# Attention and slot FFN in one kernel: the start of the first head reordered, its weights' and values' low parts moved among its scores

## The chip, the cores and the metric

The kernel runs on one core of a Trainium2 chip. The metric is the device time of one launch in microseconds, median of three runs.

## The reference

Attention over 8 batches of 1024 tokens with 8 heads of width 128, a residual and layer norm, a soft mixture of slots with its residual and layer norm behind it. Everything is fp32.

```python
q, k, v = (einsum('bim,mhd->bhid', x, w) for w in (wq, wk, wv))
q, k = rope(q), rope(k)                       # even*cos - odd*sin, even*sin + odd*cos
s = einsum('bhid,bhjd->bhij', q, k) / 128     # masked above the diagonal
o = einsum('bhij,bhjd->bhid', softmax(s), v)
x = layernorm(x + einsum('bhid,hdm->bim', o, wo))
x = layernorm(x + slot_ffn(x, gamma_x, gamma_slot, slot_embeds, w1, w2))
```

## The kernel before, in words

One block computes attention for 64 heads (8 batches x 8), a second block the FFN. The change lies in the first block and there in what precedes head 0 and in the step of head 0.

**Number format.** Matmuls run on fp32r operands in two parts: a high part (a copy rounded to fp32r, made by ScalarE with `ACT.Copy`, "hi") and a low part (the original less the high part, a subtraction on VectorE or GpSimd, "lo"). `matmul_split` (lines 53 to 57) is three matmuls: hi x hi, hi x lo, lo x hi. x, the projection weights, k, q, the values and the turned probabilities are all split so.

**A head.** k and q are projected from x (L55 to L57 into `ps_slot`), copied to SBUF (`raw_k` L516, `raw_q` L527 into `unrot`), and rotated: a product with the cosine table (`mul_cos_k` on GpSimd L417, `mul_cos_q` on VectorE L668, half by half), a swap of the upper and lower 64 partitions by two transfers on SyncE's queue (`swap`, L340), a product of the swapped copy with the sine table (`mul_sin`, GpSimd L423), a sum (`rotate_add`, GpSimd L431), then high part (`split_hi`, ScalarE L534) and low part (`split_lo`, GpSimd L439). For head 0 VectorE does part of it: sine product of k at L808, both sums at L813, both low parts at L819. The values are x times wv times wo, the product of the two weight matrices is made once (L1048, `wvo_all`, high part L593, low part L834), and the values of two heads come from one projection; head numbers -2 and -1 stand for those of the first heads (`split_v_hi` L541, `split_v_lo` L694). They are summed in `ps_turn` and `ps_y`, as the slots of `ps_slot` are taken.

**A step.** Scores of one head come in slots "s4", "s7", "s6", "s5", "s10", "s32", named by the row tiles in them. VectorE adds the mask and takes the negative row maximum (`rowmax`, L649), ScalarE takes exp (L506) into `probs`, TensorE turns the probabilities ("turn", L904, L916, L921, into two banks of `ps_turn`), ScalarE and VectorE split them (L551 to L562, L676 to L686), TensorE multiplies them with the values into `ps_y`. Each engine runs a fixed program, `step(head)`, which mixes the end of the head before, this head and the projection of the next. Order on each engine is order of the code; engines meet by semaphores alone.

**The start.** x of batch 0 arrives in halves on SyncE's queue (L390), then the two rotation tables (L394), which wait for x. ScalarE's queue brings the first two heads' k and q weights (L576), and, behind a wait for x, the values' and output weights (L579, L580) and the other six heads' weights (L583) into `probs`, which holds all raw weights before the first exp writes it. The six heads' weights are split into `kept.w` by ScalarE (`split_rest_hi`, L571) and VectorE (`split_rest_lo`, L801), before the first step. TensorE's first step waits for both low parts of q and k (`lo_made`) and for both of the values (`v_lo`, by `free_slot(v_lo, before, -2, -2, 2)`). Its turn "6a" waits for VectorE's low part of "7b", whose bank it takes (`turn("6a", head, ("7b", head))`).

`y_head` and `y_sum` hold a head's output and the sum over heads; both are first written when head 0's output is scaled, in step 1.

## Time and profile before

| | |
|---|---|
| median of 3 runs | 1671.52 us (1671.47 to 1673.33) |
| the profiled execution's own time | 1672.75 us |
| its span, first to last instruction | 1670.7 us |
| TensorE busy | 1625.1 us, 97% of the span, 10452 matmuls |
| GpSimd busy | 1413.7 us, 85% |
| VectorE busy | 1244.0 us, 74% |
| ScalarE busy | 1214.0 us, 73% |
| mean granted TensorE clock | 0.995 |

Busy shares are averages over the whole span. In the page's 40 slices (41.8 us each) TensorE reads 4 tenths in the first slice and 9 in nearly all the others; the granted clock reads 8 in the first and 9 (90% or more) in all others. In a timeline row, the first number is the start in us from the first instruction, the second the duration, and the bracket tells how long the engine had been idle before it and what ended that. Rows with ACTq or SPq are issues of transfers, not the transfers.

### The profile page before, as it was taken

The page shows a single profiled execution, that of the slowest core. Times are in us where ns is not written, and L with a number is a line of the kernel's source. Part 1 is how long each engine was busy: PE and PEld are TensorE (multiplying, and loading weights), DVE is VectorE, ACT ScalarE, POOL GpSimd, SP SyncE. Part 2 cuts the span into 40 slices and gives each one's busy share as a digit, 9 for nine tenths or more (in the row PEclk, how much of TensorE's full clock was granted, in tenths as well). Part 3 has the DMA queues.
Part 4 walks back from the last instruction along what each step waited for, and adds up shares of the span by engine and source line. Part 5 has one row for each costly group of instructions (what it writes and reads, how often), then busy time and mean ns, then how long its engine had stood idle before and what let it go on. Part 6 is the DMA issues. An engine that isn't in the chain of part 4 may idle for free. (4 is left out here: it accounts for less than half of the span.)

```text
span 1670.7 us, 29885 instructions
## 1 busy us (share of the span) xinstructions
PE 1625.1 (97%) x10452; PEld 1471.7 (88%) x10452; DVE 1244.0 (74%) x2899; ACT 1214.0 (73%) x2427; POOL 1413.7 (85%) x797
## 2 busy tenths in 40 slices
PE   4999999999999999999999999999999997999997
PEld 4899999999999999999999999999999986999997
DVE  5787778777877777778777877787777777677775
ACT  3877777777777777777777777777777764665664
POOL 4799989998999899998999899989998975777884
PEclk8999999999999999999999999999999999999999
DMA  5222232223222322232223222322232323123212
GB/s 151 77 76 75 77 99 71 74 75 98 74 75 74 100 73 75 74 99 76 77 77 102 77 77 77 102 77 76 77 89 76 89 77 102 45 67 96 68 33 58
DMA packets 69763, 134.10 MB, mean 80 GB/s; under 512 B 19312, under 2 KB 38000, under 8 KB 69616
## 3 DMA queue, kind: packets, MB, share of 16 engines
q1 hardware_dynamic: 67856, 130.10, 28.9%
q10 hardware_dynamic: 1760, 2.10, 0.4%
q8 instruction: 85, 1.39, 0.4%
q14 instruction: 62, 0.51, 0.1%
HBM read 56.36 MB, written 8.70 MB: 39 GB/s over the span
## 5 line engine op out<-in xcount | busy, mean ns | idle before, releaser
L506 ACT ACTIVATE probs<-ps_slot,neg_max 128x640 f32<-128x640 f32 (+7 forms) x512 | 381.1, 746 | 154.2 <-DVE neg_max L649 154.2
L649 DVE CUSTOM_DVE_ANT_0 ps_slot<-ps_slot,causal 128x640 f32<-128x640 f32 (+7 forms) x512 | 383.0, 769 | 132.7 <-PE ps_slot L57 132.4
L904 PE MATMUL ps_turn<-ident,probs 128*128 128x128 f32 x2048 | 279.2, 274 | 2.3 <-DVE pt_high L676 1.2
L55 PE MATMUL ps_slot<-k,q 128*128 128x512 f32 (+4 forms) x768 | 274.9, 358 | 6.5 <-DVE v L694 5.1
L57 PE MATMUL ps_slot<-k,q 128*128 128x512 f32 (+4 forms) x768 | 264.9, 345 | 0.0
L56 PE MATMUL ps_slot<-k,q 128*128 128x512 f32 (+4 forms) x768 | 263.1, 343 | 0.0
L904 PEld LDWEIGHTS ps_turn<-ident,probs 128*128 128x128 f32 x2048 | 232.8, 140 | 21.8 <-issue 2.1
L676 DVE TENSOR_TENSOR pt_split<-ps_turn,pt_split 128x512 fp32r<-128x512 f32 x256 | 175.3, 685 | 93.4 <-ACT pt_split L551 93.4
L439 POOL TENSOR_TENSOR q<-rot_q,q 128x1024 fp32r<-128x1024 f32 x63 | 152.2, 2416 | 52.6 <-ACT q L534 52.6
L423 POOL TENSOR_TENSOR swapped_k<-swapped_k,rope 128x1024 f32<-128x1024 f32 x63 | 152.4, 2420 | 42.6 <-DMA swapped_k<-unrot_k 42.5
L417 POOL TENSOR_TENSOR rot_k<-unrot_k,rope 128x1024 f32<-128x1024 f32 x64 | 154.7, 2417 | 16.4 <-ACT unrot_k L516 13.8
L55 PEld LDWEIGHTS ps_slot<-k,q 128*128 128x128 f32 x768 | 146.6, 191 | 20.8 <-issue 6.9
L423 POOL TENSOR_TENSOR swapped_q<-swapped_q,rope 128x1024 f32<-128x1024 f32 x64 | 159.2, 2487 | 6.1 <-DMA swapped_q<-unrot_q 6.1
L431 POOL TENSOR_TENSOR rot_k<-rot_k,swapped_k 128x1024 f32<-128x1024 f32 x63 | 151.8, 2409 | 9.0
L56 PEld LDWEIGHTS ps_slot<-k,q 128*128 128x128 f32 x768 | 146.4, 191 | 14.1
L431 POOL TENSOR_TENSOR rot_q<-rot_q,swapped_q 128x1024 f32<-128x1024 f32 x63 | 150.5, 2389 | 9.0
L57 PEld LDWEIGHTS ps_slot<-k,q 128*128 128x128 f32 x768 | 145.7, 190 | 13.9
L439 POOL TENSOR_TENSOR k<-rot_k,k 128x1024 fp32r<-128x1024 f32 x63 | 152.0, 2413 | 1.8 <-ACT k L534 1.8
L551 ACT ACTIVATE pt_split<-ps_turn 128x512 fp32r<-128x512 f32 x256 | 147.0, 603 | 1.9 <-PE ps_turn L904 1.9
L455 POOL TENSOR_TENSOR y_sum<-y_sum,y_head 128x1024 f32<-128x1024 f32 x55 | 132.0, 2400 | 18.7 <-issue 18.4
L1268 POOL TENSOR_TENSOR comb<-logits,row_b 128x512 f32<-128x512 f32 x64 | 96.8, 1551 | 48.4 <-DMA row_b<-r_rows 48.3
L676 DVE TENSOR_TENSOR pt_high<-ps_turn,pt_high 128x512 fp32r<-128x512 f32 (+2 forms) x192 | 100.5, 551 | 46.5 <-ACT pt_high L551 46.5
(198 smaller groups left out, 4426.1 us busy)
## 6 DMA issues: line engine op xcount, KB each, us to landing
swapped_k<-unrot_k SPq DMA_DIRECT2D x128, 256.0 KB, 3.6
swapped_q<-unrot_q SPq DMA_DIRECT2D x128, 256.0 KB, 3.6
inv_b<-inv_rows SPq DMA_DIRECT2D x64, 512.0 KB, 4.7
y_t<-y_sum SPq DMA_DIRECT2D x8, 512.0 KB, 5.4
x_raw<-y_t SPq DMA_DIRECT2D x8, 512.0 KB, 4.1
unrot_q<-in_L_attn_x SPq DMA_DIRECT2D x8, 512.0 KB, 5.4
row_b<-r_rows SPq DMA_DIRECT2D x16, 256.0 KB, 3.6
x_raw<-x_cols SPq DMA_DIRECT2D x7, 512.0 KB, 5.3
```

What stands on the lines that cost most here:

```text
L55: pe.matmul(out, stat_hi, mov_hi, start=start, stop=False, skip_group_check=True)
L56: pe.matmul(out, stat_hi, mov_lo, start=False, stop=False, skip_group_check=True)
L57: return pe.matmul(out, stat_lo, mov_hi, start=False, stop=stop, skip_group_check=True)
L417: pool.tensor_tensor(rot[1][:, :], unrot[1][:, :], kept.rope[:, 0, :], ALU.mult).then_inc(cos_made[1], 1)
L423: pool.tensor_tensor(swapped[which][:, :], swapped[which][:, :], kept.rope[:, 1, :], ALU.mult).then_inc(sin_made[which], 1)
L431: pool.tensor_tensor(rot[which][:, :], rot[which][:, :], swapped[which][:, :], ALU.add).then_inc(rotated[which], 1)
L439: pool.tensor_tensor(out[:, 1, :], rot[which][:, :], f32(out[:, 0, :]), ALU.subtract)\
L506: act.activation(probs_tile(t), score_tile(name, head, i), ACT.Exp, scale=-1.0, bias=neg_max[:, head.par, t:t + 1], accum_out=sums[:, head ...
L551: last = act.activation(hi, src, ACT.Copy)
L649: dve.tensor_tensor_reduce(tile, tile, causal[:, T - WIDTH[t]:T], -1.0, UNSEEN, ALU.add, ALU.min, neg_max[:, head.par, t:t + 1]).then_inc( ...
L676: last = dve.tensor_tensor(lo, src, f32(hi), ALU.subtract)
L904: last = pe.transpose(bank[:, at:at + P], probs_tile(t)[:, j * P:(j + 1) * P], ident[:, :])
```

## The change

It does six things, all before or in the first step:

- SyncE issues the rotation tables right behind x, without a wait.
- ScalarE loads its table by a small Exp (of a constant into `inv`, which is overwritten later), waits for x half by half and splits it, and issues the values' and output weights after that.
- The six other heads' k and q weights are loaded into `y_head` and `y_sum`, issued after the copy of q of head 0; their high parts are made in step 0 between exp of "s6" and the high part of head 1's k, their low parts in step 0 on VectorE after the row maxima of "s6" and of "s5".
- VectorE makes the low part of k before the sum of q, then the low part of q and the cosine product of head 1's q; the values' low parts come behind these and in step 0, behind the row maximum of "s7".
- ScalarE copies q of head 1 before the high part of the second values.
- TensorE's order is the same; its waits for the values' low parts move from the first scores to the first turn (one) and to step 1 (both).

```diff
@@ sync
-            sp.wait_ge(first_x_landed[1], 16)
             for i, table in enumerate((rope_c, rope_s)):
                 sp.dma_start(kept.rope[:, i, :], table).then_inc(rope_landed[i], 16)
@@ scalar
+        rest_raw = {"k": y_head, "q": y_sum}
...
-            act.wait_ge(first_x_landed[1], 16)
-            act.dma_start(w_raw["v"], wv.rearrange("d h m -> d (h m)")).then_inc(w_landed["v"], 16)
-            act.dma_start(w_raw["o"].rearrange("p (h m) -> p h m", h=H), wo.rearrange("h d m -> d h m"))\
-               .then_inc(w_landed["o"], 16)
-            for n, w in (("k", wk), ("q", wq)):
-                act.dma_start(w_raw[n][:, FIRST_HEADS * D:], w[:, FIRST_HEADS:H, :].rearrange("m h d -> m (h d)"))\
-                   .then_inc(rest_landed, 16)
+            act.wait_ge(consts, 1)
+            act.activation(inv[:, 0, :], kept.minus_half[:, :], ACT.Exp)
             for half in range(2):
                 act.wait_ge(first_x_landed[half], 16)
                 act.activation(kept.x_t[0][:, 0, half_cols(half)], kept.x_raw[:, half_cols(half)], ACT.Copy)\
                    .then_inc(first_x_hi, 1)
+            act.dma_start(w_raw["v"], wv.rearrange("d h m -> d (h m)")).then_inc(w_landed["v"], 16)
+            act.dma_start(w_raw["o"].rearrange("p (h m) -> p h m", h=H), wo.rearrange("h d m -> d h m"))\
+               .then_inc(w_landed["o"], 16)
             first, second = Head(0, 0, heads), Head(0, 1, heads)
             raw_k(first)
             raw_q(first)
+            for n, w in (("k", wk), ("q", wq)):
+                act.dma_start(rest_raw[n][:, 0:(H - FIRST_HEADS) * D], w[:, FIRST_HEADS:H, :].rearrange("m h d -> m (h d)"))\
+                   .then_inc(rest_landed, 16)
             act.wait_ge(wvo_made, 1)
             act.activation(wvo_part(0), both_y, ACT.Copy).then_inc(wvo_hi, 1)
             split_hi(1, first)
             raw_k(second)
             split_v_hi(first.step(-2))
             split_hi(0, first)
+            raw_q(second)
             split_v_hi(first.step(-1))
-            raw_q(second)
-            split_rest_hi("k", WK_HI, 1.0)
-            split_rest_hi("q", WQ_HI, 1.0 / P)
...
                 exp("s6", head)
+                if is_step(head, 0):
+                    split_rest_hi("k", WK_HI, 1.0)
+                    split_rest_hi("q", WQ_HI, 1.0 / P)
                 split_hi(1, after)
@@ vector, step
                 rowmax("s7", head)
+                if is_step(head, 0):
+                    split_v_lo(before)
...
                 rowmax("s6", head)
+                if is_step(head, 0):
+                    split_rest_lo("k", WK_HI, WK_LO, 1.0)
...
                 rowmax("s5", head)
+                if is_step(head, 0):
+                    split_rest_lo("q", WQ_HI, WQ_LO, 1.0 / P)
@@ vector, start
+            first_split_lo(1)
             first_add(0)
-            first_split_lo(1)
+            first_split_lo(0)
+            mul_cos_q(second)
             split_v_lo(first.step(-2))
-            first_split_lo(0)
-            split_v_lo(first.step(-1))
-            mul_cos_q(second)
-            split_rest_lo("k", WK_HI, WK_LO, 1.0)
-            split_rest_lo("q", WQ_HI, WQ_LO, 1.0 / P)
@@ tensor, step
+                if is_step(head, 1):
+                    pe.wait_ge(v_lo, 2)
                 weigh_high(before, (0, 1))
-                free_slot(v_lo, before, -2, -2, 2)
+                if not is_step(head, 0):
+                    free_slot(v_lo, before, -2, -2, 2)
...
+                if is_step(head, 0):
+                    pe.wait_ge(v_lo, 1)
                 turn_shared(before, head)
```

VectorE from the product of the two weight matrices to the first row maxima, before (`rot` are the rotated k and q, `w_all` the six heads' weights):

```order
L813 TENSOR_TENSOR rot_k<-rot_k,swapped_k 128x1024 [waits cos_made_k,sin_made_k]
L834 TENSOR_TENSOR wvo_all<-ps_y,wvo_all 128x1024 [waits wvo_hi]
L813 TENSOR_TENSOR rot_q<-rot_q,swapped_q 128x1024 [waits cos_made_q,sin_made_q]
L819 TENSOR_TENSOR k<-rot_k,k 128x1024 [waits hi_made_k]
L694 TENSOR_TENSOR v<-ps_turn,v 128x1024 [waits v_hi]
L819 TENSOR_TENSOR q<-rot_q,q 128x1024 [waits hi_made_q]
L694 TENSOR_TENSOR v<-ps_y,v 128x1024 [waits v_hi]
L668 TENSOR_TENSOR rot_q<-ps_slot,rope 128x512 [waits filled_q,lo_made_q]
L668 TENSOR_TENSOR rot_q<-ps_slot,rope 128x512 [waits raw_made_q]
L801 SCALAR_TENSOR_TENSOR w_all<-probs,w_all 128x6x128 [waits rest_hi] x2
L649 ISA ps_slot,neg_max<-ps_slot,causal 128x640 [waits filled_s4,consts]
```

And now:

```order
L827 TENSOR_TENSOR k<-rot_k,k 128x1024 [waits hi_made_k]
L821 TENSOR_TENSOR rot_q<-rot_q,swapped_q 128x1024 [waits cos_made_q,sin_made_q]
L827 TENSOR_TENSOR q<-rot_q,q 128x1024 [waits hi_made_q]
L670 TENSOR_TENSOR rot_q<-ps_slot,rope 128x512 [waits filled_q,lo_made_q]
L670 TENSOR_TENSOR rot_q<-ps_slot,rope 128x512 [waits raw_made_q]
L696 TENSOR_TENSOR v<-ps_turn,v 128x1024 [waits v_hi]
L651 ISA ps_slot,neg_max<-ps_slot,causal 128x640 [waits filled_s4,consts]
```

The low part of k stands before the sum of q, the low part of q before both low parts of the values, and the two weight parts have left the place before the first row maximum.

VectorE in step 0, now, from the row maximum of "s7" on (lines 651 are row maxima, 730 the weights' low parts, 678 the probabilities' low parts):

```order
L651 ISA ps_slot,neg_max<-ps_slot,causal 128x1024 [waits filled_s7]
L651 ISA neg_max 128x1
L696 TENSOR_TENSOR v<-ps_y,v 128x1024 [waits v_hi]
L688 TENSOR_TENSOR pt_high<-ps_turn,pt_high 128x128 [waits turn_hi]
L651 ISA ps_slot,neg_max<-ps_slot,causal 128x896 [waits filled_s6]
L730 SCALAR_TENSOR_TENSOR w_all<-y_head,w_all 128x6x128 [waits rest_hi]
L651 ISA ps_slot,neg_max<-ps_slot,causal 128x768 [waits filled_s5]
L730 SCALAR_TENSOR_TENSOR w_all<-y_sum,w_all 128x6x128 [waits rest_hi]
L678 TENSOR_TENSOR pt_high<-ps_turn,pt_high 128x4x128 [waits turn_hi]
```

The second values' low part and the two weight parts now stand between the row maxima and the low part of "7b".

ScalarE's start, now (line 582 splits x, 591 loads the six heads' weights):

```order
L576 DMA probs<-in_L_attn_wk 128x256
L576 DMA probs<-in_L_attn_wq 128x256
L579 ACT_TABLE_LOAD
L579 ACTIVATE inv<-minus_half 128x8 [waits consts]
L582 ACTIVATE x_t<-x_raw 128x512 [waits first_x_landed0]
L582 ACTIVATE x_t<-x_raw 128x512 [waits first_x_landed1]
L584 DMA probs<-in_L_attn_wv 128x1024
L585 DMA probs<-in_L_attn_wo 128x8x128
L516 ACTIVATE unrot_k<-ps_slot 128x1024 [waits filled_k]
L527 ACTIVATE unrot_q<-ps_slot 128x512 [waits filled_q]
L527 ACTIVATE unrot_q<-ps_slot 128x512 [waits cos_made_q]
L591 DMA y_head<-in_L_attn_wk 128x768
```

Before, the four transfers of weights stood ahead of the table load and of x's split.

## Rows read from the trace of the kernel before

**Rows 1.** Busy times in one long stretch: us, then busy (x instructions) per engine, clock.

```profile
60.00:1340.00 1280.00, 1280.00 (x8003) 1156.13 (x8003) 967.27 (x2075) 990.06 (x2076) 1153.34 (x486) 1.00 0.30 81
```

**Rows 2.** Timeline of the start, all engines, 5 to 12 us.

```profile
5.35 0.36 ACTq L579 DMA_DIRECT2D probs<-in_L_attn_wv  x1
...
5.84 0.43 DVE L794 SCALAR_TENSOR_TENSOR w_all<-probs,w_all 128x256 fp32r<-128x256 f32 x1
...
8.34 1.28 ACT L587 ACT_TABLE_LOAD   x1 [8.34 <-issue]
9.63 1.15 ACT L587 ACTIVATE x_t<-x_raw 128x512 fp32r<-128x512 f32 x2
10.29 1.29 DVE L826 TENSOR_TENSOR x_t<-x_raw,x_t 128x512 fp32r<-128x512 f32 x2 [4.03 <-ACT x_t L587]
...
11.13 0.77 PE L55 MATMUL ps_slot<-x_t,w_all 128*128 128x512 f32 x1 [11.13 <-DVE x_t L826]
```

**Rows 3.** The same timeline, k and q of head 0 and GpSimd beside them.

```profile
21.73 2.52 POOL L423 TENSOR_TENSOR swapped_q<-swapped_q,rope 128x1024 f32<-128x1024 f32 x1 [4.12 <-DMA swapped_q<-unrot_q]
...
22.05 1.06 ACT L534 ACTIVATE k<-rot_k 128x1024 fp32r<-128x1024 f32 x1 [3.08 <-DVE rot_k L813]
...
25.43 1.22 DVE L819 TENSOR_TENSOR k<-rot_k,k 128x1024 fp32r<-128x1024 f32 x1
...
26.73 2.35 POOL L417 TENSOR_TENSOR rot_k<-unrot_k,rope 128x1024 f32<-128x1024 f32 x1 [2.47 <-DVE k L819]
...
27.70 2.46 DVE L819 TENSOR_TENSOR q<-rot_q,q 128x1024 fp32r<-128x1024 f32 x1
...
29.03 3.35 POOL L423 TENSOR_TENSOR swapped_k<-swapped_k,rope 128x1024 f32<-128x1024 f32 x1
```

**Rows 4.** Durations of two VectorE lines over the whole run, ns min/median/max.

```profile
L801 DVE SCALAR_TENSOR_TENSOR w_all<-probs,w_all x2: 946/1690/2435, 33.3 to 35.6; 128x768 fp32r<-128x768 f32 x2
...
L712 DVE TENSOR_TENSOR x_t<-x_raw,x_t x14: 689/2218/2394, 82.3 to 1117.2; 128x512 fp32r<-128x512 f32 x14
```

**Rows 5.** The same timeline, first scores to the turn "6a".

```profile
31.21 1.27 DVE L668 TENSOR_TENSOR rot_q<-ps_slot,rope 128x512 f32<-128x512 f32 x2
...
31.39 0.61 PE L55 MATMUL ps_slot<-k,q 128*128 128x320 f32 x1 [5.05 <-DVE v L694]
...
32.42 1.57 ACT L571 ACTIVATE w_all<-probs 128x768 fp32r<-128x768 f32 x2
32.52 2.38 POOL L431 TENSOR_TENSOR rot_k<-rot_k,swapped_k 128x1024 f32<-128x1024 f32 x1
...
33.28 3.31 DVE L801 SCALAR_TENSOR_TENSOR w_all<-probs,w_all 128x768 fp32r<-128x768 f32 x2 [0.80 <-ACT w_all L571]
...
36.51 0.82 DVE L649 CUSTOM_DVE_ANT_0 ps_slot<-ps_slot,causal 128x640 f32<-128x640 f32 x1
36.91 2.36 POOL L423 TENSOR_TENSOR swapped_q<-swapped_q,rope 128x1024 f32<-128x1024 f32 x1 [2.01 <-DMA swapped_q<-unrot_q]
...
37.42 0.79 ACT L506 ACTIVATE probs<-ps_slot,neg_max 128x640 f32<-128x640 f32 x1 [3.44 <-DVE neg_max L649]
...
38.36 0.33 PE L921 MATMUL ps_turn<-ident,probs 128*128 128x128 f32 x1 [2.47 <-ACT probs L506]
...
45.55 0.89 PE L904 MATMUL ps_turn<-ident,probs 128*128 128x128 f32 x6 [1.18 <-DVE pt_high L676]
```

**Rows 6.** Busy times by stretch as in rows 1; the granted clock is the third last.

```profile
31.00:36.00 5.00, 4.50 (x12) 3.44 (x12) 4.20 (x5) 2.06 (x3) 3.76 (x2) 0.51 0.48 112
...
40.00:42.00 2.00, 2.00 (x6) 1.57 (x6) 1.16 (x2) 0.60 (x3) 1.78 (x1) 0.50 0.04 8
```

**Rows 7.** Stretches again (last two: DMA share, GB/s), and an issue with us to landing.

```profile
8.00:9.00 1.00, 0.00 (x0) 0.00 (x0) 0.00 (x0) 0.66 (x1) 0.00 (x0) 1.00 1.02 422
...
19.00:20.00 1.00, 1.00 (x6) 0.84 (x5) 0.46 (x1) 0.00 (x0) 0.00 (x0) 1.00 1.02 266
...
probs<-in_L_attn_wq ACTq DMA_DIRECT2D x1, 384.0 KB, 8.4
```

More of the change, by code:

```diff
@@ L571, in split_rest_hi @@
                 act.activation(kept.w[:, FIRST_HEADS:H, part, :],
-                               w_raw[n].rearrange("p (h d) -> p h d", h=H)[:, FIRST_HEADS:H, :],
+                               rest_raw[n][:, 0:(H - FIRST_HEADS) * D].rearrange("p (h d) -> p h d", d=D),
                                ACT.Copy, scale=scale).then_inc(rest_hi, 1)
@@ L723, in split_slots, with split_rest_lo @@
                                          ALU.mult, ALU.subtract).then_inc(se_lo, 1)
+            def split_rest_lo(n, hi, lo, scale):
+                raw_w = rest_raw[n][:, 0:(H - FIRST_HEADS) * D].rearrange("p (h d) -> p h d", d=D)
+                dve.wait_ge(rest_hi, ("k", "q").index(n) + 1)
+                dve.scalar_tensor_tensor(kept.w[:, FIRST_HEADS:H, lo, :], raw_w, scale,
+                                         f32(kept.w[:, FIRST_HEADS:H, hi, :]), ALU.mult, ALU.subtract)\
+                   .then_inc(w_lo[n], 1)
             def step(head):
@@ L796, in split_first_w @@
                    .then_inc(w_lo[n], 1)
-            def split_rest_lo(n, hi, lo, scale):
-                raw_w = w_raw[n].rearrange("p (h d) -> p h d", h=H)[:, FIRST_HEADS:H, :]
-                dve.wait_ge(rest_hi, ("k", "q").index(n) + 1)
-                dve.scalar_tensor_tensor(kept.w[:, FIRST_HEADS:H, lo, :], raw_w, scale,
-                                         f32(kept.w[:, FIRST_HEADS:H, hi, :]), ALU.mult, ALU.subtract)\
-                   .then_inc(w_lo[n], 1)
             def first_sin_k():
```

## The prediction

> **What bounds the kernel now.** I read the busy table of long stretches first. From 60 to 1340 us TensorE is busy 1280 of 1280 us at its full clock, while VectorE, ScalarE and GpSimd have room [rows 1]. Nothing there waits for a date of the start, so a microsecond saved before that stretch is a microsecond at the end, and the change touches only what lies before it. Then the timeline of the start. TensorE's first matmul is at 11.13 [rows 2], it stands still from about 26.3 to 31.39, and its last wait on the way to the steady part ends at 45.55, where it goes on with head 0's "6a" turn [rows 5]. I forecast two dates: first scores (31.39 now) and that turn (45.55 now).
>
> **The change, part by part.** Sums are made against the profiled execution (span 1670.7, execution 1672.75, which is 1.23 above the median of 1671.52); the saving is taken off the median. Dates "after" are mine.
>
> *x split as it lands, table at once.* Both halves of x have landed at 5.35, when ScalarE issues the transfer that waits for them. It then issues four, loads its table (1.28) and splits x only at 9.63; VectorE's part starts at 10.29 and TensorE 0.84 later [rows 2]. After, table and split are done by about 5.9. VectorE still has q's first weights to split, until 5.84 + 0.43 = 6.27 [rows 2], so it starts on x at 6.27 instead of 10.29: **4.02 us earlier**, first matmul near 7.1. Bounds: the rotation tables now follow x at once and share the engines with q's first weights. Those landed at about 5.5; they may come 0.0 to 0.6 later, and that goes one for one into this date. I take 0, since the tables stand behind x in their own queue. The values' and output weights are issued about 6 instead of 5.35; TensorE wants them near 12.0, and a wait there of a microsecond meets an idle stretch, so nothing.
>
> *The six other heads' weights come later.* Their transfers (768 KB) are now issued right behind the copy of q, when the half swap of q has just been issued. One queue alone moved 266 GB/s (19 to 20 us), two together 422 (8 to 9 us) [rows 7]. If two queues share 422 evenly, the swap (2 x 256 KB) needs 2.5 us for what takes 2.0 alone. Bounds: 0 and 3.9 us (the same weights took 8.4 us to land in company [rows 7], a swap 4.4). I take 0.3, as the pairing at 8 to 9 us is nearest. GpSimd then starts on q's sine product at 21.73 - 4.02 + 0.3 = 18.0.
>
> *The low parts of k and q, reordered.* These VectorE operations read two inputs from SBUF, and here the trace has a warning. The k low part took 1.22 with GpSimd idle; q's took 2.46: it began at 27.70, GpSimd's product ran until 29.08, and the rest is 1.1; GpSimd's next operation then took 3.35 instead of 2.4 [rows 3]. The first weight low part took 2.44 and the second 0.95, the first beside a GpSimd addition until 34.90; the x low parts took up to 2.39 [rows 4, 5]. So whoever comes second waits for the whole operation of the other. The Trainium skill states that rule ("SBUF — State Buffer", section "Who interferes with whom"): a VectorE instruction with two SBUF inputs and a GpSimd one that reads SBUF exclude each other, by order of issue. The trace agrees; without the rule the sum would be the second rival's. With these waits:
> - k: its sine product and sum keep their 4.02, high part 18.03 to 19.1. The low part finds GpSimd busy from 18.0 to 20.4 and ends at 20.4 + 1.1 = 21.5.
> - q: sum 21.4 to 22.6 (GpSimd's cosine product of head 1 waits for it and runs 22.6 to 25.0), high part 22.7 to 23.75, low part behind GpSimd, 25.0 + 1.1 = 26.1.
> - The scores no longer wait for the values' second low part, so **first scores at 26.15 instead of 31.39: 5.2 earlier**.
>
> *Step 0.* VectorE takes the cosine of head 1 (1.27, to 27.3), the values' low part (1.2, to 28.45), then the row maximum of tile 4 (0.8) at 28.4; exp (0.8 + 0.2), and the turn of tile 4 at 30.2 instead of 38.36: 8.1 earlier [rows 5]. This is the largest lead: two weight low parts (3.31) [rows 5] have left the way and the gap before the scores is shorter. Then it is given back. Tile 7's maximum and exp run 29.4 to 31.8, the values' second low part stands before tile 6's maximum, and exp of tile 6 ends at 34.2 (each of these 1.0 to 1.2). ScalarE now splits the weights (1.57 [rows 5], 34.15 to 35.7), and head 1's k comes after. VectorE's k weight low part starts at 35.0. GpSimd: the swap of head 1's q, copied at 27.3, lands 4.4 later, product to 34.1, sum to 36.4; the low part ends at 36.4 + 0.9 = 37.3. Tile 5's maximum to 38.2. GpSimd's next (k low part) has 37.3 to 39.6, so the q weight low part ends at 40.5; then the first piece of turn "7b" (0.6), and TensorE gets its bank at **41.15 instead of 45.55: 4.4 earlier**. Against an undisturbed 0.95 each, the two weight low parts take 2.8 more here. Bounds of this step: 1.1 less if the weights' parts fall into gaps of GpSimd, 1.2 more if one meets a whole operation.
>
> *TensorE's clock.* It had idled 5.05 us before 31.39, and the granted clock of 31 to 36 was 0.51, about 1.2 GHz; at 40 to 42 it was 0.50, although the engine was busy, behind 2.5 idle us before 38.36 [rows 5, 6]. Now TensorE runs out of work near 35.9 and waits to 41.15, 5.2 us, so I expect 1.2 GHz once more, but in a stretch where TensorE itself is the bound: half of 3 us (the shorter low stretch) to half of 4.5 (the longer) are lost, 1.5 to 2.2; the other bound is 0, if the clock holds. I take 1.5, the shorter, for part of it falls in the wait. The low clock of the scores in exchange may vanish; that is in no term, since VectorE's chain sets the dates there.
>
> Sum: 4.4 - 1.5 = **2.9 us faster**, 1671.5 - 2.9 = **1668.6**. About 0.2%, 3.3 us, is what a measurement of this kernel can tell from no change, so this is a gain just under it.
>
> **Rivals.**
> 1. *The order on GpSimd flips.* If q's swap lands after k's low part has begun at 19.1, that is 1.4 us later than undisturbed, k goes first, GpSimd runs q's sine product to 22.7 and head 1's cosine product straight on to 25.0, and q's sum waits for it: 26.1. High part 27.15; GpSimd meanwhile does the sine product of head 1's k until 28.5, and q's low part ends at 29.6. Scores at 29.65, 3.5 later than forecast: 0.6 slower than before, **1672.1** (1671.5 to 1672.7). For it: the trailing weights share the engines with just this swap. "DMA: Bandwidth & Descriptors" of the Trainium skill, section "Issuing engines are not separate DMA queues", says that queues of several engines end on the same DMA engines; rows 7 show that two together still move more than one. Against it: 1.4 is nearly three times the 0.5 worked out for even shares. Chance 0.13.
> 2. *No exclusion worth the name.* If the four low parts run in their 0.95 to 1.2, k ends 20.3, q 23.9, scores 24.0, and the turn comes 7 us earlier: less 1.5 of clock, **1666.0**. Against it: rows 3 and 4. Chance 0.10, with the case that the parts fall into gaps and the clock holds.
> 3. *Slower.* The swap of q waits behind the weights altogether and lands 3.9 us late, as the 8.4 of rows 7 would have it. q's sine product to 24.1, cosine to 26.4, sum 27.5, sine of k to 29.9, q's low part 31.0: scores at 31.05 as before, but step 0 still holds the weights' low parts and the cold turn, 15.0 us against 14.2 and 1.5 of clock: 2.0 slower, **1673.5**. It decides from about 2.5 us of delay on; beyond 5 it would cost over 0.2%. Chance 0.07.
> 4. *The start is not earlier.* q's first weights land so late behind the tables that x's split gains 2 instead of 4: **1670.5**. Chance 0.05. It lies in the range.
>
> **How the numbers follow.** The forecast has 0.65. Its own range: clock loss 0 to 2.2 and first weights 0 to 0.6 late, steps of GpSimd +-1.1: gains of 1.0 to 4.6. The range adds rival 1's nearer half: 1666.8 to 1671.6, leaving out rival 2, half of 1 and 3. Faster by over 0.2%: four tenths of the forecast (0.26, where the clock holds or the low parts find gaps) and rival 2: 0.36. Slower by over 0.2%: the tail of rival 3: 0.03. Within: 0.61.
>
> **What would show it.** x's high part at 5 to 6 and the first matmul near 7.1. q's sine product on GpSimd before k's low part, and k's low part near 2.4 long. q's low part near 2.3. Scores at 26.2. Weight low parts over 1.5 each inside step 0. Turn "6a" near 41.2 behind some 5 idle us, then matmuls of 0.43 per 512 columns for about 3 us. First scores later than 28 would make the forecast wrong by rival 1; low parts of 1.2, or a full clock after the wait, by rival 2.

## The result, and the profile after it

The change was forecast to save 2.9 us; it cost about 2 (1.97 by the medians, 2.3 by the ratio).

| | before | after |
|---|---|---|
| median of 19 runs each, on the same chips | 1672.37 us | 1674.34 us |
| ratio after / before | | 1.0014, 95% interval 1.0007 to 1.002 |
| the profiled execution's own time | 1672.75 us | 1674.33 us |
| its span | 1670.7 us | 1672.2 us |
| mean granted TensorE clock | 0.995 | 0.991 |

The loss of 0.14% is real, as the interval lies above 1, but less than the 0.2% that the prediction took as the limit of what can be told. The three runs of before that the forecast was set against (1671.52) were a little below the median of 19.

Three dates tell where it came from: TensorE's first scores, its turn "6a", and a **mark** behind it, the first group of seven turns in step 1, from where TensorE is full. I use the mark in every run below, since behind it the programs are alike: from the mark to the last projection of the attention, near 1340 us, it is 1288.1 us in all thirteen kernels of this document.

| us | first matmul | first scores | turn "6a" | mark | span |
|---|---|---|---|---|---|
| before | 11.13 | 31.39 | 45.55 | 53.77 | 1670.7 |
| forecast | 7.1 | 26.15 | 41.15 | 50.87 | |
| after | 7.07 | 30.24 | 45.92 | 55.44 | 1672.2 |

(The forecast's mark is 53.77 less the forecast saving of 2.9.) The first matmul came where it was expected. Of its 4.06 us of lead 1.15 were left at the scores, none at turn "6a", and at the mark the program was 1.67 late. The busy row of the long stretch answers to [rows 1]: nothing there took the delay up.

```profile
60.00:1340.00 1280.00, 1280.00 (x8004) 1156.12 (x8003) 967.22 (x2074) 990.05 (x2076) 1152.89 (x486) 1.00 0.30 81
```

The timeline of the changed kernel, all engines, from the start to the mark; the columns are those of [rows 2]. It answers to [rows 2, 3, 5].

```profile
4.40 0.63 ACT L582 ACTIVATE x_t<-x_raw 128x512 fp32r<-128x512 f32 x1 [1.24 <-DMA x_raw<-x_cols]
...
5.39 0.63 ACT L582 ACTIVATE x_t<-x_raw 128x512 fp32r<-128x512 f32 x1 [0.36 <-DMA x_raw<-x_cols]
...
5.90 0.43 DVE L809 SCALAR_TENSOR_TENSOR w_all<-probs,w_all 128x256 fp32r<-128x256 f32 x1
6.24 1.29 DVE L834 TENSOR_TENSOR x_t<-x_raw,x_t 128x512 fp32r<-128x512 f32 x2
...
7.07 0.77 PE L55 MATMUL ps_slot<-x_t,w_all 128*128 128x512 f32 x1 [7.07 <-DVE x_t L834]
...
12.10 0.35 ACTq L591 DMA_DIRECT2D y_head<-in_L_attn_wk  x1
12.49 0.50 ACTq L591 DMA_DIRECT2D y_sum<-in_L_attn_wq  x1
...
13.20 1.12 SPq L341 DMA_DIRECT2D swapped_q<-unrot_q  x2
...
18.75 1.06 ACT L534 ACTIVATE k<-rot_k 128x1024 fp32r<-128x1024 f32 x1 [3.18 <-DVE rot_k L821]
...
19.84 1.23 DVE L827 TENSOR_TENSOR k<-rot_k,k 128x1024 fp32r<-128x1024 f32 x1
...
20.52 2.80 POOL L423 TENSOR_TENSOR swapped_q<-swapped_q,rope 128x1024 f32<-128x1024 f32 x1 [6.95 <-DMA swapped_q<-unrot_q]
...
23.28 2.33 POOL L417 TENSOR_TENSOR rot_k<-unrot_k,rope 128x1024 f32<-128x1024 f32 x1
23.35 3.35 DVE L821 TENSOR_TENSOR rot_q<-rot_q,swapped_q 128x1024 f32<-128x1024 f32 x1 [2.28 <-POOL swapped_q L423]
25.57 3.32 POOL L423 TENSOR_TENSOR swapped_k<-swapped_k,rope 128x1024 f32<-128x1024 f32 x1
26.73 1.06 ACT L534 ACTIVATE q<-rot_q 128x1024 fp32r<-128x1024 f32 x1 [4.05 <-DVE rot_q L821]
...
27.82 2.16 DVE L827 TENSOR_TENSOR q<-rot_q,q 128x1024 fp32r<-128x1024 f32 x1 [1.12 <-ACT q L534]
...
30.24 0.60 PE L55 MATMUL ps_slot<-k,q 128*128 128x320 f32 x1 [7.19 <-DVE q L827]
...
40.30 1.04 DVE L730 SCALAR_TENSOR_TENSOR w_all<-y_head,w_all 128x768 fp32r<-128x768 f32 x1 [1.90 <-ACT w_all L571]
...
42.02 2.34 POOL L439 TENSOR_TENSOR k<-rot_k,k 128x1024 fp32r<-128x1024 f32 x1 [1.49 <-ACT k L534]
...
42.15 3.03 DVE L730 SCALAR_TENSOR_TENSOR w_all<-y_sum,w_all 128x768 fp32r<-128x768 f32 x1
...
45.10 1.14 DVE L678 TENSOR_TENSOR pt_high<-ps_turn,pt_high 128x512 fp32r<-128x512 f32 x2
...
45.92 1.51 PE L909 MATMUL ps_turn<-ident,probs 128*128 128x128 f32 x6 [4.63 <-DVE pt_high L678]
...
55.44 0.93 PE L909 MATMUL ps_turn<-ident,probs 128*128 128x128 f32 x7
```

Read it from the top. x is split at 4.40 and 5.39, VectorE follows at 6.24, TensorE at 7.07. Then look at the bracket of the row at 20.52: GpSimd waited 6.95 us for the half swap of q. The copy of q had ended at 13.17, so the swap landed 7.35 us behind it; before, it was 4.48 (17.25 to 21.73 [rows 3]). The three rows of issues show that the swap was not even first: ScalarE issued both transfers of weights at 12.10 and 12.49, while its copy of q was still running, and SyncE, which waits for the end of the copy, issued the swap at 13.20. Meanwhile k's low part had run (19.84, undisturbed in 1.23), so GpSimd's product began after it. At 23.28 GpSimd goes straight on to head 1's cosine product, and the sum of q, which is on the path, begins 0.07 later and takes 3.35 instead of 1.23: it waits for the whole of the other. q's low part at 27.82 meets a third product. Last, the q weights' low part (3.03) lies over a GpSimd operation of 2.34, and TensorE waits 4.63 us behind it at 45.92.

The stretches of the changed kernel; the last three columns are the granted clock, the DMA share and GB/s. They answer to [rows 6, 7].

```profile
16.00:17.00 1.00, 1.00 (x6) 0.70 (x4) 0.77 (x1) 0.00 (x0) 0.00 (x0) 1.00 1.06 410
17.00:18.00 1.00, 0.24 (x2) 0.00 (x0) 0.97 (x2) 0.00 (x0) 0.00 (x0) 1.00 1.10 280
18.00:19.00 1.00, 0.00 (x0) 0.00 (x0) 1.00 (x2) 0.25 (x1) 0.00 (x0) 1.00 0.92 217
19.00:20.00 1.00, 0.09 (x1) 0.10 (x1) 1.00 (x2) 1.00 (x2) 0.00 (x0) 1.00 0.12 33
25.00:35.00 10.00, 4.76 (x14) 4.07 (x15) 7.30 (x8) 3.96 (x7) 7.07 (x3) 0.50 0.23 57
42.00:49.00 7.00, 3.08 (x15) 3.11 (x16) 5.53 (x11) 3.38 (x10) 2.34 (x1) 0.51 0.00 0
```

The DMA engines are full until 19, at 410 GB/s from 16 to 17 and at 217 from 18 to 19, when the end of the weights (the second transfer lands 6.6 us after its issue, about 19.1) and the swap are left. A tail follows: a share of 0.12 from 19 to 20 is on average two of sixteen engines still at work. The swap's landing, at 20.52, lies behind it. TensorE's clock is at 1.2 GHz (0.50) from 25 to 35 and again from 42 to 49. The issues of transfers on the page, with KB and median us to landing, give 5.0 and 6.6 for the six heads' weights, where [rows 7] have 8.4.

```profile
y_head<-in_L_attn_wk ACTq DMA_DIRECT2D x1, 384.0 KB, 5.0
y_sum<-in_L_attn_wq ACTq DMA_DIRECT2D x1, 384.0 KB, 6.6
```

### The profile page after: what moved, and what is told of

It is laid out like the page before. It is cut to its first block and busy times, and to the rows that moved or that the text cites. A ratio compares the mean times of both kernels' runs of the same rounds, so it can differ in the third digit from the quotient of the medians.

```text
span 1672.2 us, 29888 instructions
## 1 busy us (share of the span) xinstructions
PE 1626.0 (97%) x10452; PEld 1473.0 (88%) x10452; DVE 1246.4 (75%) x2899; ACT 1214.6 (73%) x2428; POOL 1413.8 (85%) x797
```

## The experiments

A name in brackets (e1 to e11) is that of a run in the table below.

**The theory.** (A) The six heads' weights, issued beside the half swap of q, delay its landing by about 3 us. (B) Since it lands late, VectorE's k low part, now ahead of q's sum, gets in front of GpSimd's product; GpSimd then always has an operation ready at the moment when q's sum is released, and the sum waits. (C) The weights' low parts in step 0 hold turn "6a", and the wait of some 5 us costs the clock. The rivals: the order of the low parts alone does it, whenever the swap lands (against A); or the loss is all in step 0 (C without A and B).

Each row: what the profile of the run shows, the median of its timed runs beside that of before on the same chip, and the ratio with its 95% interval (11 timed runs each; 10 for e5 and e7, 6 for e9, 5 for e8). "On the change" means that the edit is made to the changed kernel.

| run | scores | "6a" | mark | span | median / before | ratio |
|---|---|---|---|---|---|---|
| weights later (e1) | 26.00 | 40.99 | 50.90 | 1668.2 | 1671.75 / 1673.61 | 0.9990 (0.9981 to 0.9999) |
| sum first (e2) | 27.35 | 43.60 | 54.36 | 1672.8 | 1673.88 / 1673.61 | 1.0003 (0.9994 to 1.0011) |
| weights' low parts later (e3) | 29.31 | 41.55 | 51.16 | 1668.8 | 1672.51 / 1673.61 | 0.9993 (0.9984 to 1.0002) |
| early x alone (e4) | 33.38 | 45.67 | 53.92 | 1671.7 | 1672.41 / 1673.61 | 0.9993 (0.9984 to 1.0002) |
| weights' transfer alone (e5) | 32.33 | 46.73 | 56.46 | 1673.8 | 1674.62 / 1673.92 | 1.0006 (0.9997 to 1.0015) |
| e1, clock kept (e6) | 25.92 | 41.27 | 49.50 | 1667.0 | 1669.50 / 1673.92 | 0.9976 (0.9967 to 0.9985) |
| e1 and e2 (e7) | 26.28 | 41.96 | 51.64 | 1669.6 | 1671.41 / 1673.92 | 0.9987 (0.9978 to 0.9996) |
| all mended (e8) | 24.44 | 35.27 | 45.79 | 1664.3 | 1666.65 / 1673.92 | 0.9963 (0.9950 to 0.9975) |
| e8, low parts behind "5b" (e9) | 24.38 | 35.22 | 44.47 | 1662.7 | 1665.34 / 1671.27 | 0.9954 (0.9939 to 0.9970) |
| early x, clear transfers (e10) | 27.57 | 42.72 | 50.92 | 1665.4 | 1667.53 / 1671.27 | 0.9976 (0.9968 to 0.9985) |
| the change, clock kept (e11) | 30.34 | 45.57 | 53.80 | 1669.7 | 1672.37 / 1671.27 | 1.0004 (0.9996 to 1.0013) |

**Weights later.** Their transfers are issued behind the high part of q. On the change:

```diff
             raw_q(first)
-            for n, w in (("k", wk), ("q", wq)):
-                act.dma_start(rest_raw[n][:, 0:(H - FIRST_HEADS) * D], ...)
...
             split_hi(0, first)
+            for n, w in (("k", wk), ("q", wq)):
+                act.dma_start(rest_raw[n][:, 0:(H - FIRST_HEADS) * D], ...)
             raw_q(second)
```

> The changed kernel, but the other six heads' weights are issued behind the high part of q instead of behind its copy. Theory (flip): these transfers made q's swap land 2.8 us late, k's low part went first and q's sum waited behind head 1's cosine product. Without them: swap landed near 17.7 instead of 20.5, q's sum starts by 21.6 instead of 23.35 and is about 1.2 long instead of 3.35, first scores near 26.2 instead of 30.24, turn 6a near 41.5 instead of 45.92, time about 4 us below the change (2 below before). Rival (step 0): what costs is the weights' low parts and the clock in step 0, the start has slack; then first scores move but turn 6a moves by less than 1 us.

The timeline of this run, k and q of head 0:

```profile
17.47 2.75 POOL L423 TENSOR_TENSOR swapped_q<-swapped_q,rope 128x1024 f32<-128x1024 f32 x1 [3.89 <-DMA swapped_q<-unrot_q]
...
19.60 1.70 DVE L827 TENSOR_TENSOR k<-rot_k,k 128x1024 fp32r<-128x1024 f32 x1
...
21.23 1.21 DVE L821 TENSOR_TENSOR rot_q<-rot_q,swapped_q 128x1024 f32<-128x1024 f32 x1
21.38 3.27 POOL L417 TENSOR_TENSOR rot_k<-unrot_k,rope 128x1024 f32<-128x1024 f32 x1 [1.16 <-DVE k L827]
...
23.71 2.03 DVE L827 TENSOR_TENSOR q<-rot_q,q 128x1024 fp32r<-128x1024 f32 x1 [1.27 <-ACT q L534]
...
26.00 0.39 PE L55 MATMUL ps_slot<-k,q 128*128 128x320 f32 x1 [2.89 <-DVE q L827]
```

This is the path of the forecast, row by row: the product before k's low part, k's low part waiting for it, then the sum of q undisturbed and GpSimd's cosine product waiting instead. Scores at 26.00 (forecast 26.15), turn "6a" at 40.99 (41.15), mark 50.90 (50.87). So A and B together make the 4.24 us at the scores, and the place of two transfers alone decides between a gain of 0.1% and a loss of 0.14%. That the mark agrees to 0.03 is partly luck: from "6a" to the mark it took 9.91 us against a forecast 9.72, and the scores were 0.15 early. The rival "order alone" has fallen: the order is the same here.

**Sum first.** The change with VectorE's order of before: q's sum ahead of k's low part.

```diff
-            first_split_lo(1)
             first_add(0)
+            first_split_lo(1)
             first_split_lo(0)
```

> The changed kernel with two VectorE instructions exchanged: q's sum before k's low part, as in the kernel before. The swap still lands late (20.5). Theory (exclusion of two-input SBUF operations and GpSimd): head 1's cosine product needs k's low part, so GpSimd can't run on; q's sum near 23.0 to 24.2 undisturbed (1.2), k's and q's low parts 24.1 to 26.5, first scores near 26.6 instead of 30.24, time about 3.5 us below the change. Rival (the late swap alone sets q's date, the order is irrelevant): k's low part is now in front of q's low part, first scores not before 29.

Its timeline, from the product on:

```profile
21.11 2.38 POOL L423 TENSOR_TENSOR swapped_q<-swapped_q,rope 128x1024 f32<-128x1024 f32 x1 [7.50 <-DMA swapped_q<-unrot_q]
...
23.52 1.23 DVE L821 TENSOR_TENSOR rot_q<-rot_q,swapped_q 128x1024 f32<-128x1024 f32 x1 [4.12 <-POOL swapped_q L423]
24.66 1.22 DVE L827 TENSOR_TENSOR k<-rot_k,k 128x1024 fp32r<-128x1024 f32 x1
...
25.87 1.23 DVE L827 TENSOR_TENSOR q<-rot_q,q 128x1024 fp32r<-128x1024 f32 x1
25.96 3.37 POOL L417 TENSOR_TENSOR rot_k<-unrot_k,rope 128x1024 f32<-128x1024 f32 x1 [2.47 <-DVE k L827]
```

The swap lands even later (21.11), so A stands, and yet the scores come 2.9 us sooner than in the change: all three VectorE operations run in 1.22. The reason is in the last row. GpSimd's cosine product overwrites `rot_k`, which k's low part reads, and so waits for it; with k's low part behind the sum, the product cannot slip in front of it. This is B by itself: from the product's begin to the scores it is 6.24 us here and 9.72 in the change. At the mark only 1.1 is left of the 2.9, for step 0 lengthened from 15.68 to 16.25 and TensorE had 5.20 us of wait and a longer stretch at 0.50 (39 to 49.3); I had expected 3.5 of the whole time.

**Weights' low parts later.** Both out of the way of turn "6a", behind the row maximum of "s10". On the change:

```diff
                 rowmax("s6", head)
-                if is_step(head, 0):
-                    split_rest_lo("k", WK_HI, WK_LO, 1.0)
...
                 rowmax("s5", head)
-                if is_step(head, 0):
-                    split_rest_lo("q", WQ_HI, WQ_LO, 1.0 / P)
...
                 rowmax("s10", head, 1)
+                if is_step(head, 0):
+                    split_rest_lo("k", WK_HI, WK_LO, 1.0)
+                    split_rest_lo("q", WQ_HI, WQ_LO, 1.0 / P)
```

> The changed kernel with both weight low parts moved behind the row maxima of s10 in step 0. Theory (flip): first scores stay at 30.2; turn 6a comes near 43.0 instead of 45.92, since low part 7b then waits only for ScalarE's high part, and TensorE idles under 2 us before it, so the clock stays at 1.0 there: 3 to 4.3 us below the change. Rival (step 0 has slack elsewhere): turn 6a at 45 or later, under 1 us.

Step 0 took 12.24 us from scores to "6a" instead of 15.68: 3.4 less, and the low parts ran in 1.07 and 0.94 where no GpSimd operation was. (I had expected the clock to stay at 1.00 here; behind a wait of 2.02 us at "6a" it was at 0.50 until 44.7.) So C is a cost of its own, apart from A and B, and both rivals that want one cause alone are out. This run also shows how narrow the flip is. The two rows of its timeline:

```profile
21.16 2.37 POOL L423 TENSOR_TENSOR swapped_q<-swapped_q,rope 128x1024 f32<-128x1024 f32 x1 [7.65 <-DMA swapped_q<-unrot_q]
...
21.33 3.29 DVE L826 TENSOR_TENSOR k<-rot_k,k 128x1024 fp32r<-128x1024 f32 x1
```

The swap of k, too, was late here (17.72 instead of 16.23), so GpSimd's product was 0.17 ahead of k's low part, as the forecast had it. The scores came at 29.31 all the same: a late swap costs about 3 us by either order. This is the program of the change up to the scores, and so is e11, where k's swap landed at 15.46: the landings differ from one execution to the next.

**Early x alone**, without moving any weights, on the kernel before: tables without a wait, x split by ScalarE ahead of its four transfers (the loop of the split is moved, so it goes from its old place).

```diff
@@ sync
-            sp.wait_ge(first_x_landed[1], 16)
@@ scalar
-            act.wait_ge(first_x_landed[1], 16)
+            act.wait_ge(consts, 1)
+            act.activation(inv[:, 0, :], kept.minus_half[:, :], ACT.Exp)
+            for half in range(2):
+                act.wait_ge(first_x_landed[half], 16)
+                act.activation(kept.x_t[0][:, 0, half_cols(half)], ..., ACT.Copy).then_inc(first_x_hi, 1)
```

> The kernel before with only its first part changed: rotation tables without a wait, table load and x's split before the transfers of the value, output and other weights, which keep their place behind x and in probs; all later orders as before. If the early split is worth its 4.0 us where nothing else collides: first matmul 7.1, swaps 4 us earlier, first scores near 27.4 instead of 31.39, turn 6a near 41.6 instead of 45.55, 3.5 to 4 us below before. If the transfers ahead of the swaps delay them: scores at 28 to 30, 1 to 3 us.

A miss: I expected scores at 27.4 and they came at 33.38. TensorE started at 6.86. The swaps run 4 us earlier than before, and so into the transfers of the weights, which are still on their way: the DMA engines are full from 11 to 16.5. The timeline:

```profile
17.93 1.23 DVE L808 TENSOR_TENSOR swapped_k<-swapped_k,rope 128x1024 f32<-128x1024 f32 x1 [4.85 <-DMA swapped_k<-unrot_k]
19.01 2.34 POOL L422 TENSOR_TENSOR swapped_q<-swapped_q,rope 128x1024 f32<-128x1024 f32 x1 [5.67 <-DMA swapped_q<-unrot_q]
19.20 3.25 DVE L813 TENSOR_TENSOR rot_k<-rot_k,swapped_k 128x1024 f32<-128x1024 f32 x1
```

Both swaps land within 1.1 us of each other, and k's sum, which stands ahead of everything, waits out q's product. The scores were 2.0 later than before with TensorE 4.3 earlier. So the early start is worth nothing unless the weights' transfers are moved as well, to where no swap is in flight.

**Weights' transfer alone**, on the kernel before: into `y_head` and `y_sum`, issued behind the copy of q and read from there by the splits, the rest as before.

```diff
-            for n, w in (("k", wk), ("q", wq)):
-                act.dma_start(w_raw[n][:, FIRST_HEADS * D:], ...)
...
             raw_q(first)
+            for n, w in (("k", wk), ("q", wq)):
+                act.dma_start(rest_raw[n][:, 0:(H - FIRST_HEADS) * D], ...)
```

> The kernel before, with only the six heads' weight transfers moved: behind the copy of q, into the head and sum buffers; all splits and orders as before. Theory: the two swaps alone already keep the 16 engines 0.9 to 1.0 busy, so 768 KB beside them have no free room. Swap of q lands near 24.5 instead of 21.73 (copy's end 17.25 plus 7.2), and first scores come 2 to 3 us later than 31.39. Rival (two queues add up, as the 422 GB/s of two loads suggested): swap by 22.3, scores within 0.6 of 31.39.

```profile
22.82 2.37 POOL L424 TENSOR_TENSOR swapped_q<-swapped_q,rope 128x1024 f32<-128x1024 f32 x1 [7.26 <-DMA swapped_q<-unrot_q]
```

ScalarE has two issues fewer ahead of x's split, so TensorE's first matmul came at 9.09, 2.04 us earlier than before, and the copy of q ended at 14.87. The swap landed 7.95 behind it, against 4.48: **3.5 us for A alone**, with no other order on VectorE, GpSimd or TensorE. It took back the 2.04 and more: scores 0.94 later, "6a" 1.18, mark 2.7. The last 1.5 go with the clock, at 0.50 from 47 to 50, where before had 1.00 behind an equal wait of 1.18 us. From SyncE's issue of q's swap to its landing it took 4.46 us before, 4.3 in e8, e9 and e10, 4.5 to 5.1 in e1, e6 and e7, which keep the weights away from it; 7.3 in the change, 7.4 in e11, 7.7 in e2, 7.9 here and 8.35 in e3, which have them beside it. (In e4 it took 6.1, beside the transfers of the start.) So A costs 2.9 to 3.9. In all five the weights were issued 0.6 to 1.1 us ahead of the swap. No run issues them just behind it, so how much of A comes from their being in front is not shown.

**The clock.** Two runs, on e1 and on the change, fill TensorE's wait before turn "6a" with 18 matmuls whose result nothing reads (`ps_y` is overwritten from its start afterwards):

```diff
                 weigh_low(before)
+                if is_step(head, 0):
+                    pe.wait_ge(v_lo, 2)
+                    for _ in range(18):
+                        pe.matmul(ps_y[:, 0, :], kept.x_t[0][:, 0, 0:P], kept.x_t[0][:, 0, 0:BANK], start=True, stop=True, ...)
                 turn("6a", head, ("7b", head))
```

> The kernel e1_rest_late with 18 matmuls that nobody reads (128x512, into the free output bank) on TensorE between turn 6b and turn 6a of step 0, where it idled 4.76 us. Theory (the low clock behind this wait costs TensorE's own work): granted clock 1.0 from 38 on, turn 6a unchanged near 41.0, the mark (seven transposes of step 1, 50.90 in e1) about 1.8 earlier, near 49.1; time 1.8 below e1. Rival (clock without effect, others set the pace): mark within 0.3 of 50.90.

> The change itself with the 18 unread matmuls of e6_clock_kept before turn 6a. Theory: of the 1.67 us by which its mark is later than before, about 1.4 are the low clock behind the 4.6 us wait; turn 6a stays near 45.9, mark near 54.0 instead of 55.44, time about 1.5 below the change, equal to before within 0.5.

The rows of e6:

```profile
36.30 4.37 PE L1046 MATMUL ps_y<-x_t 128*128 128x512 f32 x18
41.27 0.88 PE L909 MATMUL ps_turn<-ident,probs 128*128 128x128 f32 x6 [0.59 <-DVE pt_high L678]
```

On e1 turn "6a" itself came no earlier (41.27, 40.99 without), but it took 0.88 instead of 1.51, the clock stayed at 1.00, and the mark was 1.40 earlier. On the change the mark was 1.64 earlier, of which 0.35 is turn "6a". From "6a" to the mark it is 8.23 us in both, as in before (8.22); it was 9.91 in e1 and 9.52 in the change. So the term "clock", 1.5 in the forecast, is 1.7 and 1.3. In time, e6 against e1 is 0.9976 against 0.9990, e11 against the change 1.0004 against 1.0014: both the right way, each near the width of its interval.

**Weights later and sum first together**, to see whether e1 and e2 add.

> e1_rest_late and e2_sum_first together: weights issued behind the high part of q, q's sum before k's low part. If the exclusion is what is left between k and q: q's sine product 17.5 to 20.2, sum to 21.5, low parts of k and q undisturbed to 23.8, head 1's cosine product behind both; first scores near 23.9 instead of 26.0. Without that mechanism the order would not matter and scores stay near 26. The step's own waits for GpSimd may take some of it back: turn 6a between 38.5 and 40.

A miss: scores at 26.28, not at 23.9. The sum (20.16) and k's low part (21.30) ran in 1.23 and 1.22, but ScalarE was still in the high part of the values (20.80, 1.03) and made q's high part only at 21.73, and q's low part (22.81) came 0.21 behind GpSimd's cosine product and took 3.21. A fifth of a microsecond, set by a third engine, cost 2.0. So the order of e2 shields q's sum and k's low part, and leaves q's low part in a race with the cosine product, which k's low part has just released.

**All mended.** What e1 to e7 had shown, put together on the change (the code shows two of the four parts): sum first; the weights issued behind k's high part (at 18.07, as the swap of q lands); their high parts on ScalarE between the halves of head 1's copy of q; their low parts behind the row maximum of "s10".

```diff
@@ scalar, copy of q, in front of the second half
+                        if is_step(head, 1):
+                            split_rest_hi("k", WK_HI, 1.0)
+                            split_rest_hi("q", WQ_HI, 1.0 / P)
@@ scalar, start
             split_hi(1, first)
+            for n, w in (("k", wk), ("q", wq)):
+                act.dma_start(rest_raw[n][:, 0:(H - FIRST_HEADS) * D], ...)
             raw_k(second)
```

> The changed kernel with every collision found taken away: q's sum before k's low part, the six heads' weights issued behind k's high part, their high parts on ScalarE between the halves of head 1's q copy, both low parts on VectorE behind the row maxima of s10. First scores near 23.9, turn 6a near 35 to 36, idle time before it under 3 us, mark near 44 to 45, time 8 to 10 us below before. If the weights' transfers still hit a swap or land late: 4 to 6 us.

Scores at 24.44, "6a" at 35.27 behind 1.18 us, the clock never below 1.00, and the mark 8.0 earlier than before. The race of e7 was won by 0.05 us: q's low part began at 22.96, the cosine product at 23.01. One collision was left: the k weights' low part (36.10, 3.20) began 0.03 behind a GpSimd operation, and TensorE waited 2.09 us at 40.91. So the next run puts both behind the low part of "5b":

```diff
                 rowmax("s10", head, 1)
-                if is_step(head, 0):
-                    split_rest_lo("k", WK_HI, WK_LO, 1.0)
-                    split_rest_lo("q", WQ_HI, WQ_LO, 1.0 / P)
...
                 turn("5b", head)
+                if is_step(head, 0):
+                    split_rest_lo("k", WK_HI, WK_LO, 1.0)
+                    split_rest_lo("q", WQ_HI, WQ_LO, 1.0 / P)
```

> e8_all_mended with the two weight low parts one place further, behind the low part of turn 5b. In e8 the first took 3.20, since GpSimd's low part of head 1's k had begun 0.03 us before it, and TensorE then stood 2.09 at 40.91. Now they should begin near 38.8 with GpSimd idle, 1.0 each, and end by 40.8, just before TensorE's projection of head 2 needs them. Mark near 43.8 instead of 45.79, time 2 below e8, 9 to 10 below before. Rival (something else is late next, the values or head 1's q low part behind the second weight part): mark 45 or later.

TensorE's rows of this run:

```profile
24.38 0.38 PE L55 MATMUL ps_slot<-k,q 128*128 128x320 f32 x1 [2.08 <-DVE q L826]
...
35.22 0.89 PE L908 MATMUL ps_turn<-ident,probs 128*128 128x128 f32 x6 [1.18 <-DVE pt_high L678]
...
41.59 0.50 PE L55 MATMUL ps_slot<-x_t,w_all 128*128 128x512 f32 x1 [0.74 <-DVE v L696]
...
44.47 0.93 PE L908 MATMUL ps_turn<-ident,probs 128*128 128x128 f32 x7
```

The low parts now take 0.95 each and the mark is at 44.47, 9.3 us earlier than before. The time is 0.9954 of before (0.9939 to 0.9970), and the change was 1.0014, each against before on its own chip: **this version beats both**, by 0.46% and 0.6%. It, too, has q's low part only 0.05 us ahead of the cosine product (22.90 and 22.95) in the one execution that was profiled, and losing there cost 2.0 us in e7; how often its other executions lose is not known.

**Early x with clear transfers**, on the kernel before: the start of the change and the weights issued as in e8, but the order of VectorE and of step 0 as before.

> The kernel before with the early split of x and the tables without a wait, and the six heads' weights issued behind k's high part into the two free buffers; all other orders as before. This is the early start with its swaps undisturbed. If the 4.02 us are worth their face: swaps and sums 4 us earlier, first scores near 27.4, turn 6a near 41.5, mark near 49.8 instead of 53.77, 4 us below before. If the orders behind it eat it as they did in e4_early_x_alone: mark above 52.

The swaps land at 15.44 and 18.05, about 4 us earlier than before. The scores are 3.82 earlier (27.57), and one weight low part still waits (2.44). At the mark 2.85 are left; I expected 4. The stretches suggest where the last 1.0 went: TensorE now computes most scores at half clock, where before part of them ran at 1.00.

```profile
26.00:35.00 9.00, 4.95 (x14) 3.88 (x15) 7.96 (x10) 2.95 (x5) 6.94 (x3) 0.52 0.41 117
35.00:41.00 6.00, 5.54 (x23) 4.67 (x22) 2.47 (x5) 3.42 (x6) 3.10 (x3) 0.58 0.01 3
```

That the clock is the whole of it was not tried.

## Why the prediction was wrong

**The bound: right.** A microsecond before 60 us is one at the end: the delay of 1.67 at the mark is still 1.67 at the last projection of the attention (1341.86 before, 1343.53 after), and 1.5 in the span. In all twelve changed kernels the shift of the mark against 53.77 and the measured one (the ratio less 1, times the median of before) agree within 1.8 us: +1.67 and +2.3 for the change, -9.3 and -7.7 for the best version.

**x split as it lands: right.** 4.02 forecast, 4.06 measured; the lower bound on the first weights was not needed. Rival 4 did not occur.

**The weights' transfers: this step failed.** The forecast took 0.3 of delay "as the pairing at 8 to 9 us is nearest", less even than the 0.5 of its own working for even shares. It measured 2.9 to 3.9. The row for it was there, and I read its wrong column. In [rows 7] the swap alone shows a DMA share of 1.02 at 266 GB/s. The engines were *full*; the loads at 422 GB/s showed 1.02 as well. So there was no room beside the swap. The shares, summed over the stretches in which the transfers run, say what was added: the two swaps alone keep all sixteen engines busy for 3.9 us (e1, 12 to 17) and 4.2 (before, 16 to 21), swaps and weights together for 7.0 (the change, 12 to 20), 7.2 (e5, 14 to 22) and 7.7 (e3, 12 to 20). That is 3 us and more for the 768 KB, about as much as the swap was late, where at 422 GB/s they would be 1.8. Why they cost more beside the swaps than alone stays open; nor is a share near 1 one rate, for it reads 0.97 at 115 GB/s from 13 to 14 in the change. A second premise of the step was wrong as well: the weights were not issued "when the half swap of q has just been issued" but up to 1.1 us ahead of it (12.10 and 13.20). The bound of 3.9 that the step named was reached in e3; it was the choice of 0.3 inside the bounds that was wrong. The same transfers delayed k's swap, for which the forecast had no term: it landed at 16.23, where 4.02 less than before is 15.52, and k's low part began at 19.84 instead of 19.1. The sentence of the Trainium skill that the prediction cited ("DMA: Bandwidth & Descriptors", section "Issuing engines are not separate DMA queues") spoke against the 0.3: queues of several engines end on the same DMA engines. The trace agrees with the page, with a landing 7.35 us behind the copy instead of 4.48. I had set it aside because two together "move more than one", which the share column takes away.

**The order on GpSimd and the exclusion: the rule right, the branch wrong.** Every wait that the prediction drew from the rule occurred, in e1 in the forecast's order and in the change in that of rival 1: k's low part first, sine and cosine products straight on, the sum behind them, q's low part behind the product of head 1's k. Rival 1 had 29.65 for the scores, 30.24 was measured. Its condition, a swap that lands after k's low part has begun, was met by 0.68 us (20.52 against 19.84); only its chance of 0.13 hung on the 0.3 above. With 2.9 for the transfers it would have been the forecast. Rival 3 is the same branch with a swap 3.9 late; its scores (31.05) are further off than those of rival 1, but its price of 2.0 us is nearer to the 1.7 at the mark and the 2.3 in time. Rival 2 is out: in the change five operations (the sum of q, the sine product of head 1's k and the sum behind it, q's low part, a weight low part) took 0.8 to 2.1 us more than alone. The rule of the Trainium skill ("SBUF — State Buffer", section "Who interferes with whom") is that a VectorE operation with two SBUF inputs and a GpSimd one that reads SBUF contend, and that the order of issue decides who waits. The trace bears it out with 3.35 us for a sum of 1.23 that began 0.07 behind GpSimd.

**Step 0: right in its sum.** From scores to "6a" 15.0 were forecast; 15.68 were measured, 15.0 in e1. The two weight low parts took 1.04 and 3.03, 4.07 together, against the forecast's 1.9 and 2.8 more, 4.7. Not each came as forecast (over 1.5 each): the first met nothing and the second nearly a whole operation. Which of them meets GpSimd changes from run to run (1.99 and 2.22 in e1, 2.42 and 2.21 in e2), the sum little.

**The clock: right.** 1.5 forecast; 1.3 measured in the change between "6a" and the mark, 1.7 in e1. The two runs that keep it moved the mark by 1.64 and 1.40.

**The sum again with the failed term replaced.** Scores 4.09 later than forecast and step 0 0.68 longer, less 0.20 of clock (from "6a" to the mark 9.52, against 8.22 and 1.5): 4.57, which is what lies between forecast and measurement at the mark. Rival 1's time, 1672.1, was too low by 0.6 at the scores and by the 0.7 of step 0, and it was set against a median of before that with more runs is 0.85 higher.

**Left open.** How packets of the two queues alternate on an engine, and why some engines finish up to a microsecond behind the others, is in no row here. Nor did I find what decides whether k's swap lands at 16.2 (the change) or at 17.7 (e3) with the same transfers in the same order, which decides whether k's low part gets in front. The part behind the last projection took between 326.4 us (e10) and 330.4 (e8) in the thirteen profiled executions, though no run changes it; this is why a mark is used. Ratios whose interval holds 1 (e2, e3, e4, e5, e11) are not read as a gain or a loss in time.

## What to carry to other kernels

Before a transfer is moved beside one that is waited for, read how full the DMA engines are in that stretch, not how many GB/s they move: at a share near 1 there is no room, and here 768 KB that take 1.8 us at their own rate delayed the swap by 2.9 to 3.9. Read the rows of the issues too: a place behind an instruction in ScalarE's program is not a date behind its end (12.10, when the copy ended at 13.17). Where two engines exclude each other, the place of an operation in the program is worth less than what the other engine has ready at the moment of its release: an order is safe if the other's next operation waits for yours (as GpSimd's product waits for k's low part in e2), and unsafe if it depends on a landing within a few tenths of a microsecond, or if, as q's low part in e7 to e9, yours comes behind the one that releases the other. And an idle TensorE costs twice, by the wait and by the clock after it.

## What I had not expected of the hardware

- ScalarE's queue issued a transfer without waiting for the instruction in front of it to finish: at 12.10 in the change, with the second half of the copy of q still to begin (12.58) and its end at 13.17.
- Half swaps within SBUF (2 x 256 KB each) keep the sixteen DMA engines 0.8 to 1.0 busy at 176 to 266 GB/s (16 to 20 us, before); the weights' loads keep them as busy at 422.
- A queued GpSimd operation won over a VectorE one that its predecessor's end released: 23.28 against 23.35, and the loser took 2.1 us longer. In e1 it was the other way round, 21.23 against 21.38: there GpSimd's operation was the one released by VectorE's, and VectorE had its next one ready.
- Equal waits of TensorE did not give equal clocks. A wait of 1.18 us before "6a" left it at 1.00 in before and in e9; in e5 the same 1.18 was followed by 0.50 until 50, with the turn in 1.49 instead of 0.89. In e3 a wait of 2.02 was followed by 0.50 until 44.7. Their histories differ, so no threshold is read from this.
- At the very start the profile grants 1.00 while the matmuls of 512 columns follow each other every 0.43 us until about 11 in the change, and every 0.23 after it (7.64, 8.07 and on, then 11.42, 11.65). In before, which starts at 11.13, the same change comes at about 15. The granted clock of the first slices does not tell the rate there.
